# Unused expert tiles first, scatter groups one per tile, later gathers tied to TensorE's step, in a fused attention and mixture-of-experts kernel

## The chip, the cores and the metric

One core of one Trainium2 chip runs the whole program. The time is device microseconds (us) of one execution; lower is better. Timed executions are given as a median with their lowest and highest value. The profile belongs to one more execution, which has a time of its own.

## What is computed

Four sequences of 512 tokens, 512 wide (2048 tokens in all), pass through a retention-like cross-attention block and then through a mixture of experts. The part that matters here is the second one:

```python
scores = softmax(xt @ Wg.T)                       # 2048 tokens, 16 experts in 4 groups
topi   = top 4 experts inside the 2 best groups
h      = silu(xt @ W1[e].T) * (xt @ W3[e].T)      # 512 -> 352, per expert
y      = sum over the 4 chosen experts of weight * (h @ W2[e].T)
z      = the same form with shared weights, twice as wide (704)
out    = x + y + z
```

Every token goes to 4 of 16 experts, so there are 8192 pairs of token and expert.

## The kernel before

Tokens are handled in tiles of 128 rows. The expert stage has three phases of tiles, one after the other on TensorE:

- 16 tiles of all tokens through the first half of the shared weights (weight set 0; called shared-one here);
- 80 tiles of rows sorted by expert (called routed tiles; sets 1 to 16). Each expert gets as many whole tiles as its tokens need, experts follow one another, and what is left of the 80 comes last, holds no token, is computed all the same with the last expert's weights, and is read by nobody;
- 16 tiles of all tokens through the second half of the shared weights (set 17; called shared-two, S0 to S15).

Weights and activations are each split into a high and a low part, and a product is three matmuls. A tile is an `up` (24 matmuls, lines 1034 to 1036), three transposes (`tr_h`, line 860) and a `down` (9 matmuls, lines 1086 to 1088). TensorE runs, in step s, `down` of tile s-1, `tr_h` of tile s, `up` of tile s+1. Between them stand ScalarE (`silu_g`, line 770, which waits for `up`; `h_high`, 813; `x_high`, 777) and VectorE (`h_mult`, line 1331, which makes `hx` for `tr_h`; `h_low`, 1353; `x_turn`, 1340; `x_low`, 1347). Semaphore `mm1` counts finished `up`s and starts at 2, `mm2` counts finished `down`s.

The sorted order is made on the chip. During shared-one VectorE works out, in its own program between tile steps, how many tiles each expert needs (`r_places`), the slot of every pair (`r_slots`), and tables (`r_tables`, `r_packed`): which expert a tile belongs to, at which tile an expert ends, and how many stores of outputs must have landed before they may be read.

GpSimd then scatters. For each token tile t it issues four indirect DMAs (line 574; a group), one for each choice k, from `scat` in on-chip memory to `xslot_d` in DRAM. Group t waits for a step of `mm1`, for its rows to be loaded, and for group t-2 to have landed:

```python
pool.wait_ge(mm1, 2 + (30 * t + 40) // 32)
```

For t = 0 to 4 that is the end of `up` of tile t; for t = 5 and on it is tile t-1, so groups 4 and 5 wait for the same tile. SyncE loads the 16 `scat` tiles and the shared-one tiles, then waits until all 16 groups have landed, and only then runs the loop that loads routed tiles four ahead (`load_tile`, line 387), stores their outputs to `yslot_d` (`store_y`, line 411) and later writes `out`.

After the scatter GpSimd splits expert weights into high and low parts (lines 515 to 521), each as soon as the tiles that used the buffer are done (`tiles_through`, out of the table). At the end it gathers: it waits until the outputs of all tiles with tokens are stored (`stored`, out of the table; semaphores `y_stored`), and then for each token tile issues four indirect DMAs (line 607) into `gath`, which has room for four groups. Groups 1 to 3 each wait until the group before has landed; group t from 4 on waits until group t-4 has been added up (`comb`). VectorE adds them (`combine`, line 1576) between its steps of shared-two, 64 adds in all, the first right at the start of S1, about 4.5 for each step; it executes in order, so an add whose group is missing holds `x_low` and `h_mult` behind it, and with them TensorE.

Of the kernel before, what the change touches and what calls it, by code (L numbers as in the profile page):

```python
# [5 lines left out]
ALU = mybir.AluOpType  # L6
ACT = mybir.ActivationFunctionType
F32 = mybir.dt.float32
F32R = mybir.dt.float32r
BF16 = mybir.dt.bfloat16  # L10
I32 = mybir.dt.int32
U32 = mybir.dt.uint32
AX = mybir.AxisListType.X
# [9 lines left out]
NT = TOK // P  # L23
E, G, TOPG, TOPK = 16, 4, 2, 4
# [4 lines left out]
XR = 4  # L29
XG = 4  # L30
GR = 4
NW = E + N_SHARED
W13 = KT * 2 * INTER
WCOL = W13 + IC * D
# [2 lines left out]
NR = TOK * TOPK // P + E  # L37
NRP = NR + 4
# [8 lines left out]
C_IOTA, C_CAP, C_LT, C_LG, C_TILE, C_KDEC = 386, 402, 418, 674, 690, 770  # L47
# [45 lines left out]
def stream(eng, phases, aheads, ring, ramp=2):  # L93

    most, least = max(aheads), min(aheads)
    starts = [sum(ph[0] for ph in phases[:i]) for i in range(len(phases) + 1)]

    def peeled(s):
        for i, ahead in enumerate(aheads):
            for p, (tiles, looped, fns, each_pass) in enumerate(phases):  # L100
                t = s + ahead - starts[p]
                if 0 <= t < tiles and fns[i]:
                    fns[i](t, t % ring, t // ring)

    at = -max(0, most)
    for p, (tiles, looped, fns, each_pass) in enumerate(phases):
        lo = starts[p] + min(max(0, ramp - least), tiles)
        hi = max(lo, starts[p] + tiles - max(0, most))
        hi = hi - (hi - lo) % ring if looped else lo
        while at < lo:  # L110
            peeled(at)
            at += 1
        if hi > lo:
            with eng.Fori(0, (hi - lo) // ring) as j:
                if each_pass:
                    each_pass(j)
                for u in range(ring):
                    for i, ahead in enumerate(aheads):
                        t = lo - starts[p] + u + ahead
                        if fns[i]:  # L120
                            fns[i](ring * j + t, t % ring, j + t // ring)
            at = hi
    while at < starts[-1] - min(0, least):
        peeled(at)
        at += 1


def xattn_moe(nc, x, heads, wg, wo, gn, wr, wexp, tables, qdecay, out):
    outer = ExitStack()
    with outer:  # L130
# [10 lines left out]
        const = keep("const", [P, C_ALL], F32)  # L141
# [89 lines left out]
        def sb3(name, shape, dt):  # L231
            return keep(name, shape, dt)
# [6 lines left out]
        total = sb3("total", [P, 2, NT], F32)  # L239
# [4 lines left out]
        ntile = sb3("ntile", [P, 2, E], F32)  # L244
        slotf = sb3("slotf", [P, NT * TOPK], F32)
        sloti = sb3("sloti", [P, NT * TOPK], I32)
        tabf = sb3("tabf", [1, NRP + E + 1], F32)
        order = sb3("order", [1, NRP + E + 1], I32)
        packf = sb3("packf", [1, NR // XG], F32)
        packed = sb3("packed", [1, NR // XG], I32)  # L250
        ecmp = sb3("ecmp", [1, NR, E], F32)
# [10 lines left out]
        xn_d = nc.dram_tensor("xn_d", [TOK, D], F32, kind="Internal").ap()  # L262
        xslot_d = nc.dram_tensor("xslot_d", [NR * P, D], F32, kind="Internal").ap()
# [7 lines left out]
        cbf_ready, zero_ready, zeroed, y_zeroed = sem("cbf_ready"), sem("zero_ready"), sem("zeroed"), sem("y_zeroed")  # L271
# [24 lines left out]
        rt, rt_low, rt_exp, rt_sel, rt_mm, rt_slots, rt_done = (sem(n) for n in ("rt", "rt_low", "rt_exp", "rt_sel", "rt_mm", "rt_slots", "rt_done"))  # L296
# [6 lines left out]
        mm1 = sem("mm1")  # L303
# [5 lines left out]
        scattered = [sem(f"scattered{r}") for r in range(XR)]  # L309
        gathered = [sem(f"gathered{r}") for r in range(GR)]  # L310
        comb = sem("comb")
# [4 lines left out]
        def hold(eng, sem, value):  # L316


            if type(value) is not int:
                value = eng.snap(eng.to_reg(value))  # L320
            eng.wait_ge(c_loaded, 16)
            eng.wait_ge(sem, value)
# [6 lines left out]
        def _(sp):  # L329
# [52 lines left out]
            def load_tile(base, src):  # L382
                def fn(t, r, turn):
                    sp.wait_ge(x_tr, base + t + 1)
                    blocks = rows(src, t).rearrange("(c i) (q n) -> i q c n", i=Q, q=NQ)
                    for q in range(NQ):
                        sp.dma_start(xg[q * Q:(q + 1) * Q, r, :].rearrange("i (c n) -> i c n", c=NQ),
                                     blocks[:, q, :, :]).then_inc(xg_loaded[r], 16)
                return fn
# [31 lines left out]
                sp.dma_start(scat[:, r, :], rows(xn_d, t)).then_inc(scat_loaded[r], 16)  # L421

            pipeline(sp, NT, [(XG, next_tile), (3, load_scat)], ring=XG)
            for r in range(XR):
                sp.wait_ge(scattered[r], 16 * TOPK * (NT // XR))
            sp.wait_ge(y_zeroed, 16 * (NR - NT * TOPK) // 8)
            stream(sp, [(NR, True, (load_tile(NT, xslot_d), store_y, None), None),
                        (NT, False, (load_tile(NT + NR, xn_d), None, store_out), None)], (XG, -1, -3), XG)
            for p in range(2):
                sp.wait_ge(out_stored[p], 16 * (NT // 2))  # L430

# [2 lines left out]
        def _(pool):  # L434
# [131 lines left out]
            for t in range(NT):  # L566
                if t == XR:
                    pool.wait_ge(rt_slots, 2)
                pool.wait_ge(mm1, 2 + (30 * t + 40) // 32)
                pool.wait_ge(scat_loaded[t % XR], 16 * (t // XR + 1))  # L570
                if t >= 2:
                    pool.wait_ge(scattered[(t - 2) % XR], 16 * TOPK * ((t - 2) // XR + 1))
                for k in range(TOPK):
                    pool.indirect_dma_start(  # L574
                        out=xslot_d, out_offset=bass.IndirectOffsetOnAxis(ap=sloti[:, t * TOPK + k:t * TOPK + k + 1], axis=0),
                        in_=scat[:, t % XR, :], in_offset=None).then_inc(scattered[t % XR], 16)
# [24 lines left out]
            for t in range(NT):  # L601
                if 1 <= t < GR:
                    pool.wait_ge(gathered[t - 1], 16 * TOPK)
                if t >= GR:
                    pool.wait_ge(comb, TOPK * (t - GR + 1))
                for k in range(TOPK):
                    pool.indirect_dma_start(  # L607
                        out=gath[:, t % GR, k, :], out_offset=None, in_=yslot_d,
                        in_offset=bass.IndirectOffsetOnAxis(ap=sloti[:, t * TOPK + k:t * TOPK + k + 1], axis=0)).then_inc(gathered[t % GR], 16)
# [524 lines left out]
        def _(dve):  # L1134
# [187 lines left out]
            def step(ins):  # L1322
                steps[0] += 1
                ins.then_inc(rt, 1)
                dve.wait_ge(rt, steps[0])
# [82 lines left out]
            def r_places():  # L1408


                dve.wait_ge(rt_mm, 1)
                step(dve.tensor_copy(ntile[:, 1, :], ps[:, 7, NT * E:(NT + 1) * E]))
                step(dve.tensor_tensor(tc, ntile[:, 1, :, None].to_broadcast([P, E, E]),
                                       const[:, None, C_CAP:C_CAP + E].to_broadcast([P, E, E]), ALU.is_gt))
                step(dve.tensor_reduce(ntile[:, 0, :], tc, AX, ALU.add))
                step(dve.tensor_tensor(tc, ntile[:, 0, None, :].to_broadcast([P, E, E]),
                                       const[:, C_LT:C_LT + E * E].rearrange("p (a b) -> p a b", a=E), ALU.mult))
                step(dve.tensor_reduce(ntile[:, 1, :], tc, AX, ALU.add))

                step(dve.scalar_tensor_tensor(slot[:, :].rearrange("p (t e) -> p t e", t=NT), ntile[:, 1, None, :].to_broadcast([P, NT, E]),  # L1420
                                              float(P), ps[:, 7, 0:NT * E].rearrange("p (t e) -> p t e", t=NT), ALU.mult, ALU.add))
# [19 lines left out]
            def r_tables():  # L1441

                step(dve.tensor_tensor(ntile[0:1, 0, :], ntile[0:1, 0, :], ntile[0:1, 1, :], ALU.add))
                step(dve.tensor_tensor(ecmp[:, :, :], ntile[0:1, 0, None, :].to_broadcast([1, NR, E]),
                                       const[0:1, C_TILE:C_TILE + NR, None].to_broadcast([1, NR, E]), ALU.is_le))
                step(dve.tensor_reduce(tabf[:, 0:NR], ecmp[:, :, :], AX, ALU.add))
                step(dve.tensor_scalar(tabf[:, 0:NR], tabf[:, 0:NR], float(E - 1), 2.0, ALU.min, ALU.add))
                step(dve.tensor_scalar(tabf[:, NRP:NRP + E], ntile[0:1, 1, :], float(NT), None, ALU.add))  # L1450
                step(dve.memset(tabf[:, NR:NRP], 0.0))
                step(dve.tensor_scalar(ecmp[:, 0:NR // 2, 0], const[0:1, C_TILE:C_TILE + NR:2], ntile[0:1, 0, E - 1:E], 16.0, ALU.is_lt, ALU.mult))
                step(dve.tensor_reduce(tabf[:, NRP + E:NRP + E + 1], ecmp[:, 0:NR // 2, 0], AX, ALU.add))
# [198 lines left out]
```

## Time and profile before

| | us |
|---|---|
| timed executions, median (lowest to highest of 3) | 1002.01 (1000.69 to 1003.65) |
| the profiled execution, its own time | 997.2 |
| its span, first to last instruction | 995.5 |
| TensorE busy in the span | 942.9 |
| VectorE, ScalarE, GpSimd busy | 518.8, 332.9, 482.3 |

A timeline line of the profile gives start, duration, engine, line, operation, output and input, a count, and in brackets how long the engine had been idle before it and what it was released by. "remote" means that no engine's event near that time explains the release; "issue" is idle time that the profile can't put down to a wait. Ends of matmuls are modelled. The same stage is best read engine by engine for one stretch of time, since the rows of different engines name the same tile by their order alone.

### The profile page before, as it was taken

Reading aid. Unit: us, or ns where it says so; the run is one execution under the profiler, and the core shown is the slowest. Engines: PE = TensorE matmul, PEld = TensorE weight load, DVE = VectorE, ACT = ScalarE, POOL = GpSimd, SP = SyncE. Lnnn points to the kernel's source line nnn. Section 1 sums busy time; section 2 is a strip of 40 time slices with the busy share of each in tenths; the row PEclk is TensorE's granted clock in tenths of the full one; section 3 lists DMA queues with packets and bytes.
Section 4 is the critical chain, followed back from the end, with each engine's and each line's share of the span. In section 5 each row is a group of like instructions: output and inputs, shape, how many; then the busy total and the mean of one; then the engine's idle time right before and its main releaser. Section 6 shows DMA issues by size and latency. Waiting matters only on the chain.

```text
span 995.5 us, 18905 instructions
## 1 busy us (share of the span) xinstructions
PE 942.9 (95%) x5222; PEld 836.4 (84%) x5223; DVE 518.8 (52%) x1019; ACT 332.9 (33%) x711; POOL 482.3 (48%) x345
## 2 busy tenths in 40 slices
PE   7999997998869999999999999999999999998797
PEld 5767785787759988999999999999999999887686
DVE  5646668888746543333333333333333333368676
ACT  4456554454114312333333323222333332321111
POOL 1137677771355671555155545555555052316460
PEclk9999999999988999999999999999999999999999
DMA  6749985563776647434454554355555224648671
GB/s 211 253 159 400 393 312 215 195 208 113 238 248 230 219 153 257 162 95 170 172 170 169 173 174 150 108 174 174 174 174 174 84 84 138 192 134 240 195 203 60
DMA packets 120644, 187.83 MB, mean 189 GB/s; under 512 B 13600, under 2 KB 71072, under 8 KB 117920
## 3 DMA queue, kind: packets, MB, share of 16 engines
q1 hardware_dynamic: 106704, 107.96, 33.2%
q0 software_dynamic: 13904, 79.44, 23.2%
q8 instruction: 17, 0.28, 0.1%
q14 instruction: 19, 0.16, 0.1%
HBM read 111.85 MB, written 75.50 MB: 188 GB/s over the span
## 4 chain that ended last, share of the span: by engine, by line
PE 76%; DVE 10%; issue 7%; ACT 2%; DMA 2%; POOL 2%; another core or an unknown queue 1%; SPq 0%; ACTq 0%; DVEq 0%; POOLq 0%
PE ps L1034 13%; PE ps L1036 13%; PE ps L1035 13%; PE ps L1086 7%; PE ps L1088 7%; PE ps L1087 7%; PE ps L860 4%; PE ps L879 2%; DVE res L1576 2%; PE ps L880 1%; PE ps L881 1%; PE ps L901 1%; PE ps L910 1%; DVE st L1304 1%
## 5 line engine op out<-in xcount | busy, mean ns | idle before, releaser
L1034 PE MATMUL ps<-whi,xhi 128*128 (+1 forms) x896 | 301.8, 337 | 1.4 <-DVE xlo L1347 1.0
L1036 PE MATMUL ps<-whi,xlo 128*128 (+1 forms) x896 | 291.3, 325 | 0.0
L1035 PE MATMUL ps<-wlo,xhi 128*128 (+1 forms) x896 | 291.1, 325 | 0.0
L1034 PEld LDWEIGHTS ps<-whi,xhi 128*128 128x128 f32 x896 | 171.0, 191 | 2.6 <-issue 2.0
L1035 PEld LDWEIGHTS ps<-wlo,xhi 128*128 128x128 f32 x896 | 171.8, 192 | 0.0
L1036 PEld LDWEIGHTS ps<-whi,xlo 128*128 128x128 f32 x896 | 170.4, 190 | 0.0
L1331 DVE TENSOR_TENSOR hx<-ps,sg 128x352 f32<-128x352 f32 x112 | 58.7, 524 | 201.4 <-ACT sg L770 175.7
L770 ACT ACTIVATE sg<-ps 128x352 f32<-128x352 f32 x112 | 52.1, 465 | 317.2 <-PE ps L1036 277.6
L1353 DVE TENSOR_TENSOR hlo<-ps,hhi 128x384 fp32r<-128x384 f32 x112 | 62.3, 556 | 169.1 <-ACT hhi L813 164.2
L515 POOL CAST whi<-raw 128x2816 fp32r<-128x2816 f32 x16 | 40.6, 2535 | 205.1 <-PE ps L1036 205.1
L1086 PE MATMUL ps<-whi,hhi 128*128 (+1 forms) x333 | 133.1, 400 | 4.4 <-DVE hlo L1353 4.4
L1088 PE MATMUL ps<-whi,hlo 128*128 (+1 forms) x333 | 131.8, 396 | 0.0
L1087 PE MATMUL ps<-wlo,hhi 128*128 (+1 forms) x333 | 131.1, 394 | 0.0
L607 POOL DMA_INDIRECT raw<-yslot_d,sloti x64 | 63.8, 998 | 95.8 <-DVE res L1576 44.9
L517 POOL TENSOR_TENSOR wlo<-raw,whi 128x2816 fp32r<-128x2816 f32 x16 | 100.5, 6281 | 2.3 <-POOL whi L515 0.2
L820 ACT ACTIVATE ysb<-ps 128x512 f32<-128x512 f32 x80 | 48.0, 600 | 128.6 <-PE ps L1088 128.6
L574 POOL DMA_INDIRECT xslot_d<-scat,sloti x64 | 63.1, 986 | 52.0 <-issue 17.9
L813 ACT ACTIVATE hhi<-ps 128x384 fp32r<-128x384 f32 x112 | 54.6, 487 | 79.6 <-PE ps L860 53.8
L1340 DVE STREAM_TRANSPOSE ps<-xg 128x512 f32<-128x512 f32 x112 | 80.5, 719 | 1.1 <-DMA xg<-xslot_d 1.1
L860 PE MATMUL ps<-const,hx 128*128 128x128 f32 x336 | 56.3, 276 | 23.8 <-DVE hx L1331 21.8
L860 PEld LDWEIGHTS ps<-const,hx 128*128 128x128 f32 x336 | 42.8, 141 | 42.5 <-DVE hx L1331 26.2
L1086 PEld LDWEIGHTS ps<-whi,hhi 128*128 128x128 f32 x333 | 62.9, 189 | 17.9 <-DVE hlo L1353 5.4
(180 smaller groups left out, 1446.2 us busy)
## 6 DMA issues: line engine op xcount, KB each, us to landing
raw<-wexp_in POOLq DMA_DIRECT2D x18, 2176.0 KB, 9.3
xslot_d<-zero SPq DMA_DIRECT2D x10, 2048.0 KB, 21.8
xg<-xslot_d SPq DMA_DIRECT2D x320, 64.0 KB
yslot_d<-ysb SPq DMA_DIRECT2D x80, 256.0 KB
xg<-xn_d SPq DMA_DIRECT2D x128, 64.0 KB
xq<-x_in SPq DMA_DIRECT2D x16, 256.0 KB, 3.2
gate_d<-gate_out SPq DMA_DIRECT2D x16, 256.0 KB, 2.5
yslot_d<-zero SPq DMA_DIRECT2D x2, 2048.0 KB, 18.5
```

The costliest lines, as they stand in the source:

```text
L517: pool.tensor_tensor(wlo[:, p, up], raw[:, p, up], whi[:, p, up].bitcast(F32), ALU.subtract).then_inc(w13_ready, 1)
L574: pool.indirect_dma_start(out=xslot_d, out_offset=bass.IndirectOffsetOnAxis(ap=sloti[:, t * TOPK + k:t * TOPK + k + 1], axis=0), in_=scat[ ...
L607: pool.indirect_dma_start(out=gath[:, t % GR, k, :], out_offset=None, in_=yslot_d, in_offset=bass.IndirectOffsetOnAxis(ap=sloti[:, t * TOP ...
L860: mm = pe.transpose(dst[:, k * P:(k + 1) * P], src[:, k * P:(k + 1) * P], ident)
L1034: pe.matmul(ps[:, 2 + m, 0:INTER], xh, wh, start=(k == 0), stop=False)
L1035: pe.matmul(ps[:, 2 + m, 0:INTER], xh, wl, start=False, stop=False)
L1036: mm = pe.matmul(ps[:, 2 + m, 0:INTER], xl, wh, start=False, stop=(k == KT - 1))
L1086: pe.matmul(ps[:, 5 + p, :], hh, wh, start=(k == 0), stop=False)
L1087: pe.matmul(ps[:, 5 + p, :], hh, wl, start=False, stop=False)
L1088: mm = pe.matmul(ps[:, 5 + p, :], hl, wh, start=False, stop=(k == IC - 1))
L1340: dve.transpose(ps[:, p, :], xg[:, r, :].rearrange("p (c k j) -> p k c j", c=NQ, k=KT)).then_inc(x_tr, 1)
L1353: dve.tensor_tensor(hlo[:, :], ps[:, 4, 0:IC * P], hhi[:, :].bitcast(F32), ALU.subtract).then_inc(h_lo, 1)
```

## The change

- The unused tiles come first among the 80: the tables count how many of the first 79 are unused (`NL` = 15 is the most there can be), and every expert's first tile moves up by that number. They are computed with the first expert's weights. One tile, the last of the 80, stays unused at the end.
- SyncE no longer waits for the whole scatter ahead of the routed loop. Each of the first 15 loads waits for a count from the table: four groups landed for an unused tile, all 16 for one with tokens. So that the tile's number is known there, 13 more steps of its loop are written out (`ramp=13`).
- Scatter group t waits for the end of `up` of tile t, for every t.
- Gather group t from 4 on also waits for the end of `up` of shared-two tile t-3.
- VectorE gets four more short steps in `r_places` and three in `r_tables`.

As the last expert now ends at tile 79, the count in `stored` becomes that of all 80 stores.

```diff
+NL = 15
...
-            for r in range(XR):
-                sp.wait_ge(scattered[r], 16 * TOPK * (NT // XR))
+            sp.wait_ge(zeroed, 16 * (NR // 8))
+            sp.wait_ge(rt_done, 1)
+
+            def load_slots(t, r, turn):
+                if type(t) is int and t < NL:
+                    landed = sp.value_load(order[0:1, NRP + E + 1 + t:NRP + E + 2 + t], min_val=16 * TOPK, max_val=16 * TOPK * (NT // XR))
+                    for i in range(XR):
+                        hold(sp, scattered[i], landed)
+                elif type(t) is int and t == NL:
+                    for i in range(XR):
+                        sp.wait_ge(scattered[i], 16 * TOPK * (NT // XR))
+                load_tile(NT, xslot_d)(t, r, turn)
+
             sp.wait_ge(y_zeroed, 16 * (NR - NT * TOPK) // 8)
-            stream(sp, [(NR, True, (load_tile(NT, xslot_d), store_y, None), None),
-                        (NT, False, (load_tile(NT + NR, xn_d), None, store_out), None)], (XG, -1, -3), XG)
+            stream(sp, [(NR, True, (load_slots, store_y, None), None),
+                        (NT, False, (load_tile(NT + NR, xn_d), None, store_out), None)], (XG, -1, -3), XG, ramp=13)
...
-                pool.wait_ge(mm1, 2 + (30 * t + 40) // 32)
+                pool.wait_ge(mm1, 2 + t + 1)
...
                 if t >= GR:
+                    pool.wait_ge(mm1, 2 + NT + NR + t - 2)
                     pool.wait_ge(comb, TOPK * (t - GR + 1))
...
                 step(dve.tensor_reduce(ntile[:, 0, :], tc, AX, ALU.add))
+                step(dve.tensor_reduce(total[:, 0, 0:1], ntile[:, 0, :], AX, ALU.add))
+                step(dve.tensor_scalar(total[:, 1, 0:NL], const[:, C_TILE + NT * TOPK:C_TILE + NT * TOPK + NL], total[:, 0, 0:1], None, ALU.is_ge))
+                step(dve.tensor_reduce(total[:, 0, 1:2], total[:, 1, 0:NL], AX, ALU.add))
...
+                step(dve.tensor_scalar(ntile[:, 1, :], ntile[:, 1, :], total[:, 0, 1:2], None, ALU.add))
...
+                step(dve.memset(tabf[:, NRP:NRP + 1], float(NT)))
+                step(dve.tensor_scalar(tabf[:, NRP + E + 1:NRP + E + 1 + NL], const[0:1, C_TILE:C_TILE + NL], total[0:1, 0, 1:2], float(16 * (NT - TOPK)),
+                                       ALU.is_ge, ALU.mult))
+                step(dve.tensor_scalar(tabf[:, NRP + E + 1:NRP + E + 1 + NL], tabf[:, NRP + E + 1:NRP + E + 1 + NL], float(16 * TOPK), None, ALU.add))
```

## Rows read from the trace of the kernel before

**Rows 1.** Busy time by stretch: length, PE, PEld, DVE, ACT, POOL (counts), clock, DMA share, GB/s.

```profile
275.00:300.00 25.00, 15.41 (x73) 14.23 (x74) 12.27 (x27) 3.99 (x9) 14.81 (x15) 0.84 0.72 238
...
500.00:600.00 100.00, 100.00 (x574) 92.41 (x573) 36.76 (x64) 30.51 (x64) 50.62 (x19) 1.00 0.51 172
```

**Rows 2.** Timeline of ScalarE, shared-one: silu of tiles 3 to 6.

```profile
278.61 0.46 ACT L770 ACTIVATE sg<-ps 128x352 f32<-128x352 f32 x1 [9.23 <-remote]
...
286.53 0.47 ACT L770 ACTIVATE sg<-ps 128x352 f32<-128x352 f32 x1 [4.92 <-PE ps L1036]
...
298.68 0.46 ACT L770 ACTIVATE sg<-ps 128x352 f32<-128x352 f32 x1 [8.11 <-remote]
...
306.82 0.46 ACT L770 ACTIVATE sg<-ps 128x352 f32<-128x352 f32 x1 [1.34 <-PE ps L1036]
```

**Rows 3.** Timeline of TensorE: the last matmul of tile 5's up.

```profile
292.44 0.32 PE L1036 MATMUL ps<-whi,xlo 128*128 128x352 f32 x1
```

**Rows 4.** Timeline of GpSimd: twelfth scatter issue in a row; first of groups 4, 5, 6, 8.

```profile
275.59 0.96 POOL L574 DMA_INDIRECT xslot_d<-scat,sloti  x1 [0.30 <-issue]
...
287.27 0.96 POOL L574 DMA_INDIRECT xslot_d<-scat,sloti  x1 [2.65 <-issue]
...
292.36 0.97 POOL L574 DMA_INDIRECT xslot_d<-scat,sloti  x1 [0.30 <-issue]
...
298.92 0.97 POOL L574 DMA_INDIRECT xslot_d<-scat,sloti  x1 [1.77 <-remote]
...
313.31 0.97 POOL L574 DMA_INDIRECT xslot_d<-scat,sloti  x1 [1.45 <-PE ps L1036]
```

**Rows 5.** Timeline of VectorE: the first turn of a routed tile.

```profile
367.33 0.73 DVE L1340 STREAM_TRANSPOSE ps<-xg 128x512 f32<-128x512 f32 x1 [0.80 <-DMA xg<-xslot_d]
```

**Rows 6.** Timeline of VectorE: tile 1's hx, and a short step of the tables.

```profile
259.68 0.53 DVE L1331 TENSOR_TENSOR hx<-ps,sg 128x352 f32<-128x352 f32 x1 [0.74 <-ACT sg L770]
...
282.76 0.19 DVE L1449 TENSOR_SCALAR tabf<-tabf 1x80 f32<-1x80 f32 x1
```

**Rows 7.** SyncE's waits over the span: in total, times, longest.

```profile
SPq L411 <- ACT ysb L820: 267.6, 79, 7.6
```

**Rows 8.** Timeline of GpSimd: the split of the last weight set begins.

```profile
795.42 2.54 POOL L515 CAST whi<-raw 128x2816 fp32r<-128x2816 f32 x1 [23.71 <-PE ps L1036]
...
805.94 3.51 POOL L521 TENSOR_TENSOR wlo<-raw,whi 128x1536 fp32r<-128x1536 f32 x1
```

**Rows 9.** Timeline of SyncE: ninth store of a routed output from the end, and the last.

```profile
829.79 0.37 SPq L411 DMA_DIRECT2D yslot_d<-ysb  x1
...
879.56 0.36 SPq L411 DMA_DIRECT2D yslot_d<-ysb  x1
```

**Rows 10.** Timeline of GpSimd: first issue of gather groups 0 to 3.

```profile
832.69 1.01 POOL L607 DMA_INDIRECT raw<-yslot_d,sloti  x1 [23.25 <-DMA yslot_d<-ysb]
...
842.01 0.95 POOL L607 DMA_INDIRECT raw<-yslot_d,sloti  x1 [4.51 <-DMA raw<-yslot_d,sloti]
...
849.94 0.95 POOL L607 DMA_INDIRECT raw<-yslot_d,sloti  x1 [3.20 <-DMA raw<-yslot_d,sloti]
...
857.64 0.96 POOL L607 DMA_INDIRECT raw<-yslot_d,sloti  x1 [2.96 <-DMA raw<-yslot_d,sloti]
```

**Rows 11.** Timeline of ScalarE: silu of routed tiles, four steps apart.

```profile
839.44 0.46 ACT L770 ACTIVATE sg<-ps 128x352 f32<-128x352 f32 x1 [2.62 <-PE ps L1036]
...
866.09 0.47 ACT L770 ACTIVATE sg<-ps 128x352 f32<-128x352 f32 x1 [2.61 <-PE ps L1036]
```

**Rows 12.** Timeline of VectorE, shared-two: thirteenth add, hx of S4, a sum, hx of S15.

```profile
900.67 0.74 DVE L1576 SCALAR_TENSOR_TENSOR res<-raw,top,res 128x512 f32<-128x512 f32 x1
...
904.81 0.53 DVE L1331 TENSOR_TENSOR hx<-ps,sg 128x352 f32<-128x352 f32 x1 [0.89 <-issue]
...
924.76 0.69 DVE L1561 TENSOR_TENSOR res<-res,ps 128x512 f32<-128x512 f32 x1 [3.97 <-remote]
...
986.88 0.53 DVE L1331 TENSOR_TENSOR hx<-ps,sg 128x352 f32<-128x352 f32 x1 [0.28 <-ACT sg L770]
```

More of the change, by code:

```diff
@@ L246, in xattn_moe @@
         sloti = sb3("sloti", [P, NT * TOPK], I32)
-        tabf = sb3("tabf", [1, NRP + E + 1], F32)
-        order = sb3("order", [1, NRP + E + 1], I32)
+        tabf = sb3("tabf", [1, NRP + E + 1 + NL], F32)
+        order = sb3("order", [1, NRP + E + 1 + NL], I32)
         packf = sb3("packf", [1, NR // XG], F32)
```

## Prediction

> **What bounds the kernel now.** I read the stretches first, then each engine's timeline in the two stretches that differ from the rest, the scatter and the gather. In the middle TensorE is busy all the time, 574 matmul records in 100 us; at 36 for a tile that is 6.27 us a tile [rows 1]. Nothing can be won or lost there unless TensorE has to wait. Around the scatter it isn't full: 15.41 of 25 us busy, and the granted clock falls to 0.84, since after an idle stretch TensorE runs for a while at the lower of its two levels [rows 1]. So I look there for who is late.
>
> ScalarE's silu of tile 3 and of tile 5 come after idle times of 9.23 and 8.11 us that the profile puts down to "remote"; those of tiles 4 and 6 come right after their `up` [rows 2]. The `up` of tile 5 ended at 292.44 + 0.32 = 292.76 [rows 3], and its silu began at 298.68: the signal arrived 5.92 us late. What runs meanwhile is GpSimd. Before tile 3's late signal it had issued twelve indirect DMAs in a row, the last at 275.59; before tile 5's it issued group 4 at 287.27 and group 5, without a pause, at 292.36, 1.27 for each of the four between [rows 4]. From group 6 on each group waits for its own tile, 1.45 us idle in group 8 [rows 4], and no silu is late. My reading, an inference: while many indirect DMAs are queued, TensorE's signals reach the other engines late. VectorE shows the same in the gather, a sum that waited 3.97 us for nothing that can be named [rows 12].
>
> At the end the place to look is the first add of each gather group, since VectorE executes in order. There the kernel before has a head start: gathers begin at 832.69, while unused tiles still run [rows 10], because the ninth store of a routed output from the end (829.79) was the last that mattered [rows 9]. So tile 71 is the last with tokens: 72 tiles used, 8 not, and after the change 7 of these come first and one stays last.
>
> **Step 1, the scatter pacing.** Groups 0 to 4 wait for the same tiles as before, so the first stall (silu of tile 3) stays. Groups 4 and 5 no longer go together: group 5 waits for tile 5, whose `up` then ends about 6.27 us after tile 4's, which is the pattern of the groups that hurt nobody. If so the second stall goes: from tile 4's silu to tile 6's now 306.82 - 286.53 = 20.29 us, two clean steps are 12.54, gain 7.75. It is 0 if four queued DMAs do the harm already. I take 7.75: from group 6 on each burst is four and none is late.
>
> **Step 2, the unused tiles ahead.** Their loads no longer wait for the whole scatter. Behind shared-one the two phases are not overlapped anyway (`x_turn` of the first routed tile stands behind `h_low` of the last shared one). The load itself was late by only 0.80 us [rows 5]: gain 0.8, between 0 and 0.8. The scatter's last groups come a tile (6.27) later, but seven unused tiles, 7 x 6.27 = 43.9 us, lie ahead of the first load that needs them. What is queued behind GpSimd's later scatter is the first weight split; its expert also begins seven tiles later. SyncE's loads wait on a table value; behind them stand its stores. The trace shows no such register read on SyncE; it idles 267.6 / 79 = 3.4 us a tile [rows 7] and loads four tiles ahead, so 15 tiles would have to lose some 25 us together before TensorE noticed. I take 0.
>
> The last weight set is split 14.03 us after the tile before the last expert ended (795.42 to 805.94 + 3.51) [rows 8]. The last expert then has about four tiles (from 795.42 to its last store, 829.79, are 5.5 steps, of which some 1.5 lie between an `up` and its store) [rows 8, 9]. With the one unused tile that makes five steps, 31 us, of cover for 14. Cost 0.
>
> **Step 3, the tables.** Seven short steps at 0.19 us [rows 6]; the four in `r_places` (0.76) lie ahead of tile 1's `hx`, where VectorE had 0.74 idle [rows 6]. I take 0; all seven on the path would be 1.3.
>
> **Step 4, the gathers lose their head start.** This is the dear part. `stored` now counts all 80 stores, the last of which is issued at 879.56 [rows 9]. In the old run the gather followed its last needed store by 832.69 - 829.79 = 2.90 [rows 9, 10], so it begins at 882.46 on the old clock. Groups 0 to 3 are a chain, each waiting for the landing of the one before: links of 9.32, 7.93 and 7.70 [rows 10]; the fourth I take at their lower ones, 7.8. Group 3 is there at 882.46 + 9.32 + 7.93 + 7.70 + 7.8 = 915.21. Its first add stood at 900.67, and `hx` of S4 followed at 904.81 after 4.14 us, 0.89 of them idle [rows 12], so S4's `hx` comes at 915.21 + 3.25 = 918.46 instead of 904.81: **13.65 us lost**. This wait takes the place of the tile-by-tile work: VectorE stands at S1's first add with `x_low` and `h_mult` behind it, so TensorE stands too. Later groups keep ahead of their adds.
>
> A page of the Trainium skill prices this otherwise: DMA: Bandwidth & Descriptors, Anatomy of one DMA, gives a DMA issued by GpSimd some 2.0 us plus its bytes at 436 GB/s, 2.6 us for a 256 KB gather. As an estimate from it a link would be three issue intervals of about 1.27 and 2.6, 6.4 us, S4's `hx` would come at 911.3, and the sum below would end near -2.4 us. The rows' links of 7.70 to 9.32 don't agree with it.
>
> Then the late signals. From S4 to S15 the old run takes 986.88 - 904.81 = 82.07 us [rows 12], 13.1 above eleven steps of 6.27, with 44 gathers issued in that stretch. Now GpSimd runs behind, and the 48 of groups 4 to 15 go back to back: 13.1 x 48 / 44 = 14.3, **1.2 more**. Bounds: 13.1 less, if the signals were never late, and some 4 more, if unbroken bursts weigh heavier than broken ones. The new gather wait on `up` of tile t-3 I take at 0: the adds of group t-4, on which the same gather waits, end about as late.
>
> In return no gather runs beside the last routed tiles any more: four steps there took 866.09 - 839.44 = 26.65, against 25.08 [rows 11], gain 1.57.
>
> **Sum.** 13.65 + 1.2 - 7.75 - 0.8 - 1.57 = +4.7 us. The profiled execution took 997.2 with a span of 995.5, the median of the timed ones is 1002.0; the 4.8 between them I carry over. So 1001.9 for a profiled execution, **1006.7** for the median.
>
> **The rivals.** *A, the second stall stays*, because four queued DMAs and the loads beside them are enough, or because it moves to another group: without the 7.75 it is 1014.5. For it: tile 5's signal was due only 0.40 us after group 5 began (292.36 to 292.76), so group 4 may have done it alone. Against: no group after 6.
>
> *B, the gather chain is shorter.* With the routed tiles over there are no output stores beside it. If a group landed as fast after its last issue as the last store did (2.90), a link would be three intervals of 1.27 and 2.90, 6.7 us; group 3 would be there at 909.3, S4 would lose 7.7 instead of 13.65, and the sum is -1.2: 1000.8, no change. Against it stand three measured links. It decides once the mean link is under 7.3.
>
> *C, faster: the signals at the end are no longer late.* In the old run each burst began right when the adds freed a slot, in the middle of a tile; if the wait on TensorE's step, or gathers that TensorE has to wait for anyway, put bursts where no signal is due, up to 13.1 + 1.2 come back: 1006.7 - 14.3 = 992.4. The sign turns once a third of that (4.7) comes back. Against: groups 4 to 9 find their TensorE step long past, so nothing paces them.
>
> *D, it doesn't do what it says*: the count of unused tiles comes out as 0, and the order stays the old one. Then step 1 gives its 7.75, but the first routed load waits for a scatter that ends a tile later: 1002.0 - 7.75 + 6.27 = 1000.5, no change.
>
> **How the numbers follow.** Chances: forecast 0.45, A 0.22, B 0.18, C 0.13, D 0.02. About 0.3%, 3 us, is what a measurement of this kernel can tell from no change. The forecast's own range is 1003 to 1011, so 0.05 of it falls within 0.3%; faster is C, 0.13, within 0.3% is 0.18 + 0.05 + 0.02 = 0.25, slower 0.62. The range goes from 1000 (B, D) to 1017 (A with some heavier bursts) and leaves out C and the far ends, about 0.2.
>
> **What would show it.** Step 1: silu of tile 3 still about 9 us after "remote", silu of tile 5 right behind its `up`. Step 2: no wait on a DMA at the first routed `x_turn`. Step 4: the first gather about 3 us behind the last store of a routed output, VectorE waiting for gathers before the adds of groups 0 to 3, some 9 us before the first, and TensorE idle there. I am wrong if the links are near 6.7 us, if the late silu only moves on, or if the steps from S4 on take other than about 7.5 us each.

## The result, and the profile after

The changed kernel takes 1006.65 us (median; 1004.21 to 1009.66) where the kernel before, run beside it, takes 1000.06 (992.59 to 1005.09). The ratio is 1.0062, with a 95% interval of 1.0044 to 1.0079: slower by some 6 us. The profiled execution of the changed kernel took 1006.91, with a span of 1005.3.

The page after shows busy times as before, and where the time is lost. In the lines over 40 slices each digit is the busy share of a slice in tenths, and PEclk the granted clock:

```profile
PE 944.3 (94%) x5222; PEld 839.3 (83%) x5223; DVE 519.4 (52%) x1026; ACT 333.2 (33%) x711; POOL 485.9 (48%) x345
...
PE   8999997999879989999999999999999999956998
...
PEclk9999999999989999999999999999999999977999
```

TensorE is as busy as before (944.3 us against 942.9). What is new is the hole in the 36th and 37th slices, at 50 to 60% and a clock of 0.7: the start of shared-two, where the gathers now begin. Between the same instructions of both timelines (ScalarE's `silu_g`, VectorE's `hx`, the stores) the stages took:

| stage, us | before | after | difference | predicted |
|---|---|---|---|---|
| silu of tile 2 to silu of tile 15 (shared-one) | 97.05 | 89.50 | -7.55 | -7.75 |
| to the silu of the first routed tile | 10.73 | 9.86 | -0.87 | -0.80 |
| from there to the silu of S0 (80 routed tiles) | 504.81 | 503.06 | -1.75 | -1.57 |
| `hx` of S0 to `hx` of S4 | 25.73 | 44.84 | +19.11 | +13.65 |
| `hx` of S4 to `hx` of S15 | 82.07 | 79.47 | -2.60 | +1.20 |
| sum | | | +6.34 | +4.73 |

The span grew by 9.8 in these two executions. Of the rest 3.24 lie ahead of the scatter, in work that the change doesn't touch (GpSimd's memset of `hx` at 245.98, before at 242.74). It starts at 245.68 in a kernel below that shares this part with the one before (e4), and at 243.06 in one that shares it with the one after (e5): it varies from one execution to the next.

**The scatter.** ScalarE's silu of tiles 3 to 6, TensorE's last matmul of tile 3's `up`, and GpSimd's first issues of groups 3 to 6:

```profile
282.42 0.46 ACT L783 ACTIVATE sg<-ps 128x352 f32<-128x352 f32 x1 [9.24 <-remote]
289.92 0.47 ACT L783 ACTIVATE sg<-ps 128x352 f32<-128x352 f32 x1 [4.50 <-PE ps L1049]
296.53 0.47 ACT L783 ACTIVATE sg<-ps 128x352 f32<-128x352 f32 x1 [2.57 <-PE ps L1049]
303.41 0.46 ACT L783 ACTIVATE sg<-ps 128x352 f32<-128x352 f32 x1
```

```profile
275.37 0.32 PE L1049 MATMUL ps<-whi,xlo 128*128 128x352 f32 x1
```

```profile
282.66 0.97 POOL L586 DMA_INDIRECT xslot_d<-scat,sloti  x1 [2.56 <-remote]
...
290.65 0.97 POOL L586 DMA_INDIRECT xslot_d<-scat,sloti  x1 [2.22 <-issue]
...
296.77 0.97 POOL L586 DMA_INDIRECT xslot_d<-scat,sloti  x1 [1.32 <-PE ps L1049]
...
302.91 0.97 POOL L586 DMA_INDIRECT xslot_d<-scat,sloti  x1 [1.33 <-PE ps L1049]
```

Each is to be held against [rows 2 to 4]. Tile 3's silu is as late as it was: its `up` ended at 275.37 + 0.32 = 275.69, the silu began 6.73 later. Tile 5's 8.11 "remote" is gone; it comes 0.39 behind the end of its `up` (296.14). Groups 4, 5 and 6 now start 6.1 apart, 5 and 6 released by TensorE, where groups 4 and 5 stood end to end before.

One rival can be settled here: that ScalarE itself stood still. GpSimd's group 3 waits for the same `up` of tile 3 as that silu, and it too was released late, by "remote", 0.24 us behind it (282.66 and 282.42). Before it was the same, for tile 3 and for tile 5 (group 6 at 298.92, silu at 298.68 [rows 2, 4]). The same 0.24 lies between such a pair where nothing is late (307.06 and 306.82 before, group 7 and tile 6's silu). Two engines had the signal at the same moment, so it was the signal that was late.

**The gather.** SyncE's last store of a routed output, GpSimd's first issues of groups 0 to 3, and VectorE's first adds of groups 0 to 3 with `hx` of S4 and what follows it:

```profile
872.88 0.36 SPq L412 DMA_DIRECT2D yslot_d<-ysb  x1
```

```profile
875.81 1.01 POOL L620 DMA_INDIRECT raw<-yslot_d,sloti  x1 [27.46 <-DMA yslot_d<-ysb]
...
885.90 1.35 POOL L620 DMA_INDIRECT raw<-yslot_d,sloti  x1 [5.27 <-DMA raw<-yslot_d,sloti]
...
894.70 1.34 POOL L620 DMA_INDIRECT raw<-yslot_d,sloti  x1 [3.67 <-DMA raw<-yslot_d,sloti]
...
903.66 1.35 POOL L620 DMA_INDIRECT raw<-yslot_d,sloti  x1 [3.37 <-DMA raw<-yslot_d,sloti]
```

```profile
885.67 0.75 DVE L1597 SCALAR_TENSOR_TENSOR res<-raw,top,res 128x512 f32<-128x512 f32 x1 [10.39 <-DMA raw<-yslot_d,sloti]
...
894.47 0.75 DVE L1597 SCALAR_TENSOR_TENSOR res<-raw,top,res 128x512 f32<-128x512 f32 x1 [2.98 <-DMA raw<-yslot_d,sloti]
...
903.42 0.75 DVE L1597 SCALAR_TENSOR_TENSOR res<-raw,top,res 128x512 f32<-128x512 f32 x1 [3.97 <-DMA raw<-yslot_d,sloti]
...
912.39 0.75 DVE L1597 SCALAR_TENSOR_TENSOR res<-raw,top,res 128x512 f32<-128x512 f32 x1 [3.20 <-DMA raw<-yslot_d,sloti]
...
917.24 0.52 DVE L1344 TENSOR_TENSOR hx<-ps,sg 128x352 f32<-128x352 f32 x1 [1.58 <-issue]
925.24 0.69 DVE L1582 TENSOR_TENSOR res<-res,ps 128x512 f32<-128x512 f32 x1 [7.47 <-remote]
```

The first gather follows the last store by 875.81 - 872.88 = 2.93, as in [rows 9, 10], but now it is the last store of all. Each add of groups 0 to 3 waits for its group, 10.39 us the first, and four steps of shared-two take the pace of the gather: 15.20, 8.80, 10.21 and 10.63. The last row is a late signal: the sum at 925.24 waits for `down` of S3, whose last matmul ended at 916.08, 9.16 us earlier, while GpSimd issued 16 gathers end to end from 903.66 to 924.05. The windows show TensorE in it (length, PE, PEld, DVE, ACT, POOL busy with counts, clock, DMA share, GB/s):

```profile
877.00:885.00 8.00, 2.47 (x12) 1.72 (x10) 0.00 (x0) 0.46 (x1) 2.89 (x3) 0.79 0.80 197
...
907.00:909.00 2.00, 1.82 (x7) 1.82 (x8) 1.88 (x4) 0.88 (x2) 1.48 (x2) 0.50 0.90 251
```

It idles in the first, 2.47 of 8 us busy, and when work comes it does it at the lower of its two clock levels for a while: 0.50 in the second, which in the timeline ends around 912, where a matmul goes from 0.49 to 0.33 us.

### The profile page after: what moved, and what is told of

The parts are those of the page before. It is cut to its first block, busy times and chain, and to the rows that moved or that the text cites. A ratio compares the mean times of both kernels' runs of the same rounds, so it can differ in the third digit from the quotient of the medians.

```text
span 1005.3 us, 18991 instructions
## 1 busy us (share of the span) xinstructions
PE 944.3 (94%) x5222; PEld 839.3 (83%) x5223; DVE 519.4 (52%) x1026; ACT 333.2 (33%) x711; POOL 485.9 (48%) x345
## 4 chain that ended last, share of the span: by engine, by line
PE 73%; DVE 9%; DMA 5%; issue 5%; ACT 3%; another core or an unknown queue 2%; POOL 2%; SPq 0%; ACTq 0%; DVEq 0%; POOLq 0%
PE ps L1047 13%; PE ps L1049 13%; PE ps L1048 13%; PE ps L1099 7%; PE ps L1101 7%; PE ps L1100 7%; PE ps L873 4%; DMA raw<-yslot_d,sloti 1%; DMA xg<-xslot_d 1%; PE ps L914 1%; PE ps L923 1%; DVE st L1317 1%; DVE res L1315 1%; POOL raw L620 1%
## 5 line engine op out<-in xcount | busy, mean ns | idle before, releaser
L620 POOL DMA_INDIRECT raw<-yslot_d,sloti x64 | 66.7, 1041 | 67.6 <-DMA yslot_d<-ysb 27.5
```

Of the source, the lines that this page charges most:

```text
L620: pool.indirect_dma_start(out=gath[:, t % GR, k, :], out_offset=None, in_=yslot_d, in_offset=bass.IndirectOffsetOnAxis(ap=sloti[:, t * TOP ...
```

## The experiments

The theory was: (1) while GpSimd issues many indirect DMAs end to end, TensorE's signals reach the others late, so every wait that breaks the issues into fours is worth several us; (2) the order with the unused tiles first costs the head start of the gather. The rivals were that the cost lies in the bytes that these DMAs move and not in their issuing, that the new order would have removed the late silu without the scatter's new step, and that the new gather wait does nothing.

### The scatter's step alone (e1_scatter_step)

```diff
 # the kernel before
-                pool.wait_ge(mm1, 2 + (30 * t + 40) // 32)
+                pool.wait_ge(mm1, 2 + t + 1)
```

> The kernel before, with the scatter line of the change alone: group t waits for up of tile t. Theory (queued indirect DMAs make TensorE's signals late, two groups back to back are enough): silu of tile 5 follows its up at once instead of 5.92 us late, 7.75 us come back; but the old order waits for the whole scatter before the first routed load, and that now ends a tile, 6.27 us, later: together -1.5 us, ratio to before 0.9985. Rival (four queued DMAs are enough, the stall stays or moves): nothing comes back, +6.3 us, ratio 1.006.

Measured: 998.57 (995.03 to 1002.55), ratio 1.0011 (0.9985 to 1.0036), no difference. Both halves are in the trace: from silu 2 to silu 15 it takes 88.62, 8.43 less than before, and from there to the first routed silu 18.60, 7.87 more. VectorE's first turn of a routed tile shows what it waits for:

```profile
366.54 0.73 DVE L1340 STREAM_TRANSPOSE ps<-xg 128x512 f32<-128x512 f32 x1 [6.84 <-DMA xg<-xslot_d]
```

It was 0.80 in [rows 5]. Since the scatter ends a tile later, the first load waits for it. With the unused tiles ahead this wait is gone (9.86 in the table): the new order is what lets the scatter's step pay.

### The new order with the old step (e2_old_scatter_step)

```diff
 # the kernel after
-                pool.wait_ge(mm1, 2 + t + 1)
+                pool.wait_ge(mm1, 2 + (30 * t + 40) // 32)
```

> The changed kernel with the old scatter line: groups 4 and 5 wait for the same tile again, the rest of the change stays. Theory: the stall before the silu of tile 5 is back, +7.75 us against the changed kernel, so about +14.3 against before, ratio 1.014. Rival (the stall went for another reason, such as the loads or the table steps around it): no difference from the changed kernel, ratio 1.006.

Measured: 1014.14 (1011.27 to 1017.16), ratio 1.0157 (1.0117 to 1.0198), 0.0095 or 9.5 us above the changed kernel. Silu 2 to silu 15 takes 99.11, 9.61 more than with the new step, and a silu is again late in the way of [rows 2]:

```profile
301.12 0.46 ACT L783 ACTIVATE sg<-ps 128x352 f32<-128x352 f32 x1 [6.70 <-remote]
```

```profile
301.36 0.97 POOL L586 DMA_INDIRECT xslot_d<-scat,sloti  x1 [0.36 <-remote]
```

The second line is group 6, which waits for the same `up` and is again 0.24 behind the silu.

So the second stall belongs to groups that run end to end, not to the order of the tiles.

### Without the new gather wait (e3_no_gather_wait)

```diff
 # the kernel after
                 if t >= GR:
-                    pool.wait_ge(mm1, 2 + NT + NR + t - 2)
                     pool.wait_ge(comb, TOPK * (t - GR + 1))
```

> The changed kernel without the new wait of the later gathers on TensorE's step. The prediction put that wait at 0: then the ratio to before stays at 1.006. Rival, from the changed kernel's trace: from S5 to S15 it takes 65.0 us where before took 73.8, with gathers from group 10 on each started by TensorE's step; if the wait does that, it is worth some 8.8 us and without it the ratio is 1.015.

Measured: 1016.99 (1014.22 to 1021.02), ratio 1.0186 (1.0145 to 1.0228), 12.4 us above the changed kernel. S0 to S4 takes 45.42, about the same (44.84); S4 to S15 takes 91.80 against 79.47. GpSimd's last of 24 issues in a row, the next, and ScalarE's and VectorE's end of the same stretch:

```profile
934.50 0.96 POOL L619 DMA_INDIRECT raw<-yslot_d,sloti  x1 [0.30 <-issue]
945.86 0.95 POOL L619 DMA_INDIRECT raw<-yslot_d,sloti  x1 [10.40 <-DVE res L1596]
```

```profile
925.19 0.32 PE L1048 MATMUL ps<-whi,xlo 128*128 128x352 f32 x1
```

```profile
939.32 0.46 ACT L782 ACTIVATE sg<-ps 128x352 f32<-128x352 f32 x1 [13.23 <-remote]
```

```profile
939.81 0.53 DVE L1343 TENSOR_TENSOR hx<-ps,sg 128x352 f32<-128x352 f32 x1 [9.61 <-ACT sg L782]
```

S5's `up` ended at 925.19 + 0.32 = 925.51 and its silu began at 939.32, 13.81 later, not until the burst of 905.12 to 935.46 was over. The step S4 to S5 took 20.80; in the changed kernel 14.46. Of the 12.33 between the two kernels 6.34 lie in this step and the rest behind it. The four kernels here that have the wait and seven or five unused tiles ahead made this step in 14.46 to 16.97 (the changed one, e2, e6, e8), with 16 to 20 in a row. The wait is worth 12 us, not 0.

### The gather wait alone (e4_gather_wait)

```diff
 # the kernel before
                 if t >= GR:
+                    pool.wait_ge(mm1, 2 + NT + NR + t - 2)
                     pool.wait_ge(comb, TOPK * (t - GR + 1))
```

> The kernel before with the new gather wait alone. If the wait paces the gathers and so keeps TensorE's signals on time: up to 13.1 us of late signals between S4 and S15 come back, some 8.8 as in the changed kernel from S5 on: ratio 0.991. If it is met before the adds free a slot, as the prediction had it: no difference, ratio 1.000.

Measured: 992.15 (989.20 to 998.42), ratio 0.9943 (0.9918 to 0.9968), 5.7 us faster than before. S4 to S15 takes 73.79 instead of 82.07; S0 to S4 1.80 more. From group 10 on GpSimd's groups are now released by TensorE, tile by tile (first issues of groups 10, 11 and 13):

```profile
930.68 0.95 POOL L608 DMA_INDIRECT raw<-yslot_d,sloti  x1 [2.08 <-PE ps L1037]
...
937.20 1.32 POOL L608 DMA_INDIRECT raw<-yslot_d,sloti  x1 [1.79 <-PE ps L1037]
...
949.89 1.18 POOL L608 DMA_INDIRECT raw<-yslot_d,sloti  x1 [1.34 <-PE ps L1037]
```

In the kernel before, the gathers from group 5 on stood in runs of eight and once of twelve; here are first issues of groups 10 and 11 there, the second 0.56 us behind the end of group 10:

```profile
930.31 0.95 POOL L607 DMA_INDIRECT raw<-yslot_d,sloti  x1 [5.74 <-DVE res L1576]
...
935.76 0.95 POOL L607 DMA_INDIRECT raw<-yslot_d,sloti  x1 [0.56 <-issue]
```

With the wait two runs of eight are left (groups 5 and 6, 7 and 8) and fours behind them. This one line, without the rest of the change, makes the kernel faster.

### A quarter of the bytes (e7_thin_scatter)

```diff
 # the kernel before; xthin_d is [NR*P, D//4]
-                        out=xslot_d, ...
-                        in_=scat[:, t % XR, :], in_offset=None)
+                        out=xthin_d, ...
+                        in_=scat[:, t % XR, 0:D // 4], in_offset=None)
```

> The kernel before, but the scatter writes only the first quarter of each row, into a buffer of its own, and the routed tiles read zeros: the same number of indirect DMAs at the same places with a quarter of the bytes. Theory A, what is queued in bytes makes the signals late: silu of tiles 3 and 5 follow their up at once, tile 2's silu to tile 15's takes about 81.5 us instead of 97. Theory B, the number of indirect DMAs issued in a row, or GpSimd's issuing of them, does it: both stalls stay and it takes about 97.

Measured: 1001.16 in one execution; silu 2 to silu 15 takes 99.00. Both late signals stay (silu of tiles 3 and 5), and the window around the first shows the DMA engines little used:

```profile
282.14 0.46 ACT L771 ACTIVATE sg<-ps 128x352 f32<-128x352 f32 x1 [9.10 <-remote]
...
299.54 0.46 ACT L771 ACTIVATE sg<-ps 128x352 f32<-128x352 f32 x1 [5.25 <-remote]
```

```profile
276.00:280.00 4.00, 1.78 (x8) 1.12 (x6) 0.00 (x0) 0.00 (x0) 3.09 (x4) 1.00 0.38 106
```

As smaller groups land sooner, groups 4 to 6 ran end to end, twelve issues, and the step behind them took 13.33. So it isn't the bytes, nor full DMA engines (share 0.38): it goes with how many indirect DMAs are issued in a row. Each DMA still moved its 128 rows, so a count of rows isn't told apart from a count of DMAs. What in the issuing holds the signals is not shown by any run here.

### Only three unused tiles first (e5_three_first)

```diff
 # the kernel after, r_places
                 step(dve.tensor_reduce(total[:, 0, 1:2], total[:, 1, 0:NL], AX, ALU.add))
+                step(dve.tensor_scalar(total[:, 0, 1:2], total[:, 0, 1:2], 3.0, None, ALU.min))
```

> The changed kernel, but at most three of the seven unused tiles go first; four stay behind the tiles with tokens, with the last one. Theory (the loss is the gathers' lost head start, the gains are the scatter pacing and the gather wait): the gathers begin five tiles, some 31 us, earlier against the last store, groups 0 to 3 are there before their adds, S0 to S4 takes about 26 us instead of 44.8, and S4 to S15 about 74 as in the kernel before with the gather wait: against before -7.5 (scatter) -0.9 (first routed load) -6.5 (gather wait), ratio 0.985. Rival (the loss comes from the order itself, such as the weights of the first expert or the loads): it stays near 1.006.

Measured: 987.42 (984.72 to 990.26), ratio 0.9906 (0.9877 to 0.9935). Shared-one keeps its gain (89.37), the first routed silu is not late (9.86), and S0 to S4 takes 30.64 instead of 44.84, since five unused tiles at the end let the gather begin 20 us ahead of the last store. That is the price of the order, and it shows that the gain in the scatter needs few tiles ahead. What is left of it: groups 3 and 4 go end to end, eight issues, and a signal comes late:

```profile
882.46 0.96 POOL L620 DMA_INDIRECT raw<-yslot_d,sloti  x1 [0.30 <-issue]
```

```profile
887.42 0.49 ACT L826 ACTIVATE hhi<-ps 128x384 fp32r<-128x384 f32 x1 [5.29 <-remote]
```

### The scatter two tiles later (e6_scatter_two_later, e8_five_first_two_later)

If the first stall too comes from groups 0 to 2 going end to end, a later step should break them up. e6 is the kernel after, e8 has five unused tiles first as well:

```diff
-                pool.wait_ge(mm1, 2 + t + 1)
+                pool.wait_ge(mm1, 2 + t + 3)
```

> The changed kernel with each scatter group waiting for the up of tile t+2 instead of tile t, so that groups 0 to 2 no longer go back to back (this order of waits works because seven unused tiles lie ahead here). Theory: the first stall is the same thing as the second, silu of tile 3 follows its up at once, and tile 2's silu to tile 4's takes about 12.5 us instead of 20.4: 7.9 us faster than the changed kernel, ratio to before 0.998. Rival (the first stall comes from the routing steps or from code and loads at that time): it stays, ratio 1.006.

> Both together: five unused tiles first, two behind, and each scatter group waits for the up of tile t+2 (this order of waits works because unused tiles lie ahead here). Theory: no late signal at the scatter (-15.4 against before), first routed load on time (-0.9), the gathers begin three tiles, 19 us, ahead of the last store and groups 0 to 3 are ready for their adds, and the gather wait gives some 6.5: about -22 us, ratio 0.978. Rival, if the groups 0 to 3 come too late with 19 us of head start: part of the 19 us of the changed kernel is left, ratio 0.985 or more.

Measured: e6 1002.21 (1000.48 to 1005.59), ratio 1.0054 (1.0035 to 1.0073); e8 992.90 (989.80 to 1000.77), ratio 0.9965 (0.9942 to 0.9989), far from what was expected of it. In e6 the first stall is gone: silu 2 to silu 4 takes 12.53, in the changed kernel 20.43. But silu 2 to silu 15 falls by 3.16 only. The waits of 270 to 320 (in total, times, longest) name what came instead:

```profile
DVE ps L1353 <- DMA xg<-xn_d: 10.4, 5, 3.6
```

SyncE runs `load_scat`, which waits for a scatter group, and the loads of the shared-one tiles in one order, so a later scatter holds these loads. In e8 silu 2 to silu 15 falls by 3.45 only, and the five tiles ahead leave so short a head start that 20 gathers go end to end from 887.09 on; S4 to S5 takes 16.97.

### Few tiles first, gathers one tile later (e9_two_first_gather_later, e10_three_first_gather_later)

```diff
 # the kernel after, with e5's line and 2.0 (e9) or 3.0 (e10) in it
-                    pool.wait_ge(mm1, 2 + NT + NR + t - 2)
+                    pool.wait_ge(mm1, 2 + NT + NR + t - 1)
```

> Two unused tiles first instead of all seven, and the later gathers wait for one step of TensorE more (group t for the up of shared-two tile t-2). Theory (late signals come with more than one group in a row, and the head start of the gathers pays): scatter as in the changed kernel, -7.5 against before; the first routed loads cost about 1 us more than there, near 0; with six tiles of head start group 3 is issued before S1 and no two groups go together, so S0 to S4 takes about 26.5 us and S4 to S15 about 73: in all about -16 us, ratio 0.984. Rival (one step more is too late for the adds): the adds wait for gathers, S4 to S15 takes 80 or more, ratio 0.991 or more.

> Three unused tiles first, and the later gathers wait for one step of TensorE more. Against the run with three first alone (ratio 0.9906, S0 to S4 30.6 us, S4 to S15 73.8): theory: groups 3 and 4 still touch, groups 5 and 6 no longer do, so some 2 to 3 us less, ratio 0.988; rival (the wait is too late for the adds): slower than with three first alone, ratio over 0.991.

Measured: 980.17 (977.91 to 982.31), ratio 0.9798 (0.9764 to 0.9833), and 980.17 (976.54 to 980.51), ratio 0.9795 (0.9760 to 0.9829). Both beat the kernel before by 2% and the one after by more. In e9 the scatter stage takes 89.38, S0 to S4 24.83, and S4 to S15 71.22, 2.2 above eleven steps of 6.27. GpSimd's first gather, and first issues of groups 4 to 6:

```profile
842.01 1.01 POOL L620 DMA_INDIRECT raw<-yslot_d,sloti  x1 [23.07 <-DMA yslot_d<-ysb]
...
886.19 0.95 POOL L620 DMA_INDIRECT raw<-yslot_d,sloti  x1 [13.96 <-PE ps L1049]
...
892.78 0.96 POOL L620 DMA_INDIRECT raw<-yslot_d,sloti  x1 [1.88 <-PE ps L1049]
...
899.23 1.13 POOL L620 DMA_INDIRECT raw<-yslot_d,sloti  x1 [1.25 <-PE ps L1049]
```

The gather has its head start (the last store is issued at 875.15), each group of four waits for TensorE, and from S4 on steps go 5.5 and 7.5 in turn. The two kernels differ in one tile's place and not in time. e10 gained more than was expected of it (0.988), and not as expected: groups 5 and 6 still stand end to end there (892.70 to 903.36), as 3 and 4 do (880.34 to 890.52), and S3's silu begins 5.30 behind the end of its `up`:

```profile
892.21 0.47 ACT L783 ACTIVATE sg<-ps 128x352 f32<-128x352 f32 x1 [5.25 <-remote]
```

S0 to S4 took 25.92 all the same, 1.09 more than in e9: a late signal needn't cost its whole length.

A signal due inside a group of four is on time. In e9 group 4 was issued from 886.19 to 890.90; TensorE's `tr_h` of the step, ScalarE's `h_high`, which waits for it, and the group's last issue:

```profile
887.84 0.49 PE L873 MATMUL ps<-const,hx 128*128 128x128 f32 x3
```

```profile
888.37 0.49 ACT L826 ACTIVATE hhi<-ps 128x384 fp32r<-128x384 f32 x1 [1.95 <-PE ps L873]
```

```profile
889.95 0.95 POOL L620 DMA_INDIRECT raw<-yslot_d,sloti  x1 [0.30 <-issue]
```

Both kernels depend on the eight unused tiles that these inputs leave. What stays in both is the stall of tile 3's silu.

## Why the prediction was right, point by point

Direction and size came out: +4.7 foretold, 1006.65 - 1000.06 = +6.6 measured. The terms of the scatter and the small ones are near; the two of the gather were off by 5.5 and 3.8, with opposite signs. That the time itself (1006.7 foretold, 1006.65 measured) came out to a tenth is luck: the kernel before took 1000.06 beside it and not the 1002.0 that the sum starts from, and the change cost 1.9 more than foretold.

- **Step 1, the scatter pacing, -7.75.** Right: -7.55. The stall of tile 3 stayed, that of tile 5 went, as foretold. From tile 4's silu to tile 6's it is 303.41 - 289.92 = 13.49, not 12.54; the next step gives most of that back (5.51 instead of 6.24). No late signal is behind it: tile 6's silu stood 1.02 behind the end of its `up` (302.39) since ScalarE was loading an activation table just before (302.12 to 303.40). Rival A (the stall stays) is out: e2 shows that the stall comes back with the old step.
- **Step 2, the unused tiles ahead, -0.8.** Right: -0.87; VectorE's first turn of a routed tile has no wait on a load. Without the new order the same step costs 7.87 (e1), which is what rival D described, with 6.27 for it. D is out, since the first gather follows the last store of all. SyncE's waits on the table cost nothing that can be seen: the routed tiles took 503.06.
- **Step 3, the tables, 0.** From the memset to the scatter's start it takes 19.03 after and 18.76 before: 0.27, between the ends 0 and 1.3.
- **Routed tiles without gathers beside them, -1.57.** -1.75.
- **Step 4, the lost head start, +13.65.** The mechanism is the one foretold, place by place: first gather 2.93 behind the last store (2.90), first add 10.39 idle (some 9), TensorE idle with it. The size was 19.11, 5.46 more. The mis-sized term is the chain: links of 10.09, 8.80, 8.96 and (to the landing, at VectorE's add) 912.39 - 903.66 = 8.73, together 36.58, where [rows 10] gave 32.75 with 7.8 for the fourth: 3.83 more. The rows were of gathers beside routed tiles; those of the gather alone were expected to be the same or shorter (rival B), and were longer, part in the issuing (1.35 for a first issue where it was 0.95), most in the landing. Rival B fell: its links of 6.7 were nowhere. The Trainium skill (DMA: Bandwidth & Descriptors, Anatomy of one DMA) gives a DMA issued by GpSimd some 2.0 us and its bytes at 436 GB/s. None of the four links agrees with the 6.4 that the prediction estimated from it. The other 1.6 lie between group 3's add and S4's `hx`, 4.85 instead of 3.25: S4's `up` ended at 913.98, and its silu came 2.77 later, at 916.75, while GpSimd was in a burst of 16; so a late signal stands in this term too.

```profile
913.66 0.32 PE L1049 MATMUL ps<-whi,xlo 128*128 128x352 f32 x1
```

- **The late signals, +1.2, and the new gather wait, 0.** This step failed: -2.60. It took all 48 gathers to go end to end and counted the harm by their number. Two things were missed. The harm goes with the length of a burst, not with the count: a burst of 16 made a step of 14.46, bursts of 20 steps of 15.40 to 16.97 (e2, e6, e8), one of 24 a step of 20.80. (The count was misread too: between `hx` of S4 and of S15 GpSimd issued 37 gathers before, not 44, and 42 after, not 48.) And the gather wait paces: the step foretold that groups 4 to 9 find their TensorE step long past, and groups 4 to 6 did, in a row with group 3. Group 7 began at 927.49, behind group 3's last add (925.96), and from group 9 on they stand in fours, from group 10 on mostly released by TensorE's step. First issues of groups 10 and 11, after:

```profile
945.55 1.31 POOL L620 DMA_INDIRECT raw<-yslot_d,sloti  x1 [1.20 <-PE ps L1049]
...
951.67 0.95 POOL L620 DMA_INDIRECT raw<-yslot_d,sloti  x1 [1.03 <-PE ps L1049]
```

  Taken away, it costs 12.4 us (e3); put alone into the kernel before, it gains 5.7 (e4). This is rival C's mechanism. It was priced at 14.3, and its place was foretold rightly ("put bursts where no signal is due"), but as a rival against the forecast; in fact part of it happened within it. The text's bound of "some 4 more, if unbroken bursts weigh heavier" is what e3 exceeds: 91.80 - 82.07 = 9.7.

So the sum was near because a chain that was too short by 5.5 met a stage in which the late signals cost 3.8 less than foretold. That the two errors nearly cancel is luck too; the mechanism of the scatter and of the lost head start was right, that of the wait was not. The reading that carried the forecast, that many indirect DMAs in a row make TensorE's signals late, stood every test that was made of it: e2 and e3 bring the late signals back by joining groups, e4 and e9 remove them where they part the groups (in e4 two runs of eight stay, and with them S4's and S6's silu 2.79 and 2.86 late), e7 excludes the bytes. Its cause inside the chip stays open, as does a cure for the first stall, since the one tried (e6) only moved the wait to SyncE's loads.

## What to carry to other kernels

When a transfer phase begins behind the work that feeds it, price the whole chain up to the first consumer that stands still, and take the chain's links in the surroundings that they will have, not those that they had. Where one engine issues indirect DMAs for another's steps, a wait that costs nothing by its own release time can be worth much by what it keeps apart (here one line, 5.7 us). And a change of several edits is best taken apart before it is judged: here the order of the tiles took away what two waits gave, and with two or three tiles ahead instead of seven, and the gathers one step later, the kernel gained 2%.

## What the runs showed of the hardware

- Eight to 24 indirect DMAs issued end to end by GpSimd went with signals of TensorE that reached ScalarE late: by 2.79 to 5.92 us with eight (S4 in e4; tile 5 before), 6.40 and 6.73 with twelve (tile 3 before and after), 7.81 to 11.51 with 20 (S5 in e2 and e8), 13.81 with 24 (S5 in e3). Most came about when the run ended: in e3 the last issue ended at 935.46 and the silu began at 939.32, after the change 280.10 and 282.42 (tile 3). S4's silu after came inside its run, 2.77 late. GpSimd, waiting for the same `up`, had the signal 0.24 behind ScalarE. With a quarter of the bytes it stayed (9.10 and 5.25 idle), at a DMA share of 0.38.
- In fours, 6 us apart, no signal was late in this way; in e9 one that was due inside a group (`tr_h` ended at 888.33) was answered at 888.37.
- A group of four gathers, 1.27 us from issue to issue, took 8.7 to 10.1 us from its first issue to its landing with TensorE mostly waiting, longer than the 7.7 to 9.3 of [rows 10] with the routed tiles at work. Why was not tried.
- After an idle stretch of TensorE (2.47 of 8 us busy) the granted clock was 0.50 at 907 to 909, and a matmul of `up` took 0.49 us instead of 0.32.
